# A relational graph layer's loop of 34 turns written out, with two buffers per fetched row slot and edge tables kept in DRAM

## The reference, cut to what matters

```
h = relu(layernorm(x));  x = x + sage_sum(h)       # two convolutions
h = relu(layernorm(x));  x = x + relational(h)     # the layer of this change
h = relu(layernorm(x));  x = x + attention(h)      # three attention convolutions
h = relu(layernorm(x));  x = x + sage_mean(h)      # two convolutions, batch norm

def relational(feat):              # src, dst: int (103125,), sorted by dst
    h_src = feat[src]              # etypes: 0..15; weight: (16, 64, 64)
    for r in range(16):
        msg += (h_src * (etypes == r)) @ weight[r]
    return segment_sum(msg, dst)
```

## Time and profile before

| | |
|---|---|
| median of 3 runs | 2148.41 us (2145.63 to 2152.9) |
| the profiled execution, its own time | 2156.55 us |
| its span, first to last instruction | 2154.8 us |
| PE busy | 1729.2 us (80%) |
| DVE busy | 1499.3 us (70%) |
| ACT busy | 1127.3 us (52%) |
| POOL busy | 898.3 us (42%) |
| gathers (L947), 544 for the slots | 555.8 us busy, 1022 ns each, 304.1 us idle before them |

### The profile page before, as it was taken

The page is one execution under the profiler, slowest core; times in us unless marked ns, Lnnn a source line. Parts: engine busy times, 40 slices in busy tenths (PEclk is TensorE's granted clock), DMA queues, the critical chain, the costliest instruction groups (busy, mean ns, idle before and its releaser), DMA issues. The chain is left out here.

```text
span 2154.8 us, 36900 instructions
## 1 busy us (share of the span) xinstructions
PE 1729.2 (80%) x9923; PEld 873.3 (41%) x9924; DVE 1499.3 (70%) x4058; ACT 1127.3 (52%) x2235; POOL 898.3 (42%) x828
## 2 busy tenths in 40 slices
PE   2777777883688878888887888789998998999786
PEld 0222222551344434444443444465535543544354
DVE  6999997435455666666665666478886887888854
ACT  6777776212333333333343333338885886888521
POOL 1000000005666666666666666315653654455400
PEclk9999999896799898999999899869999999999898
DMA  6000000102111111111111111220000000000000
GB/s 176 0 0 0 0 0 5 69 1 64 32 33 30 29 31 30 29 30 35 30 30 31 29 31 30 47 78 2 1 1 1 1 1 1 1 1 1 16 1 16
DMA packets 29633, 50.74 MB, mean 24 GB/s; under 512 B 12820, under 2 KB 13826, under 8 KB 29054
## 3 DMA queue, kind: packets, MB, share of 16 engines
q0 software_dynamic: 17664, 18.12, 4.9%
q1 hardware_dynamic: 11890, 31.59, 4.6%
HBM read 36.58 MB, written 7.39 MB: 20 GB/s over the span
## 5 line engine op out<-in xcount | busy, mean ns | idle before, releaser
L947 POOL DMA_INDIRECT adj<-h_table,l_idx x544 | 555.8, 1022 | 304.1 <-issue 152.4
L1138 DVE TENSOR_SCALAR adj<-adj,node_key 125x1024 f16<-125x1024 f16 x825 | 373.9, 496 | 338.5 <-PE psum L1083 153.6
L1083 PE MATMUL psum<-adj,x_sb 125*128 125x512 f16 x1650 | 446.9, 413 | 136.7 <-DVE adj L1138 122.2
L1648 POOL TENSOR_TENSOR gat_ring<-gat_ring,adj 125x750 f32<-125x750 f32 (+2 forms) x225 | 310.6, 1382 | 264.1 <-ACT gat_ring L1704 261.9
L1543 DVE SCALAR_TENSOR_TENSOR gat_ring<-x_sb,gat_node,psum 125x750 f32<-125x750 f32 (+2 forms) x375 | 317.9, 861 | 60.5 <-PE psum L1781 26.3
L1011 ACT ACTIVATE l_z<-psum 128x320 f32<-128x320 f32 x204 | 89.0, 436 | 462.3 <-remote 206.8
L1083 PEld LDWEIGHTS psum<-adj,x_sb 125*128 125x128 f16 x1650 | 162.2, 104 | 356.6 <-DVE adj L1138 165.5
L393 PE MATMUL psum<-col_hot,src_hot 128*128 128x500 bf16 x808 | 204.9, 375 | 109.8 <-DVE src_hot L322 88.7
L1778 PE MATMUL psum<-gat_ring,gat_hx 125*65 125x500 f32 (+1 forms) x500 | 242.9, 575 | 16.0 <-DVE gat_ring L1554 9.5
L319 DVE TENSOR_SCALAR col_hot<-iota_h,c_tab 128x500 bf16<-128x500 f16 x808 | 227.6, 346 | 24.7 <-PE psum L393 20.1
L1701 ACT ACTIVATE gat_ring<-gat_ring,gat_node 125x750 f32<-125x750 f32 (+2 forms) x225 | 182.2, 810 | 60.5 <-DVE gat_ring L1543 58.6
(11 more groups left out here) (260 smaller groups left out, 2298.2 us busy)
## 6 DMA issues: line engine op xcount, KB each, us to landing
adj<-h_table,l_idx POOLq DMA_INDIRECT x544
adj<-key_table SPq DMA_DIRECT2D x33, 250.0 KB
adj<-adj SPq DMA_DIRECT2D x3, 1662.5 KB
adj_saved<-adj SPq DMA_DIRECT2D x1, 3840.3 KB
adj<-adj_saved SPq DMA_DIRECT2D x5, 688.2 KB
x_sb<-in_x SPq DMA_DIRECT2D x1, 781.2 KB
x_saved<-x_sb SPq DMA_DIRECT2D x1, 781.2 KB
out<-x_sb SPq DMA_DIRECT2D x5, 156.2 KB
```

What stands on the lines that cost most here:

```text
L947: pool.indirect_dma_start(out=to[:, t, :], out_offset=None, in_=table[:, :], in_offset=bass.IndirectOffsetOnAxis(ap=index[:, t:t + 1], axi ...
L1083: last = pe.matmul(psum[:, PAIR[half] + t, :], h_parts[:, k, :], select[0:P, k % SELECTS, t * GE:(t + 1) * GE], start=(k == 0), stop=(k == ...
L1138: v.tensor_scalar(select[0:P, k % SELECTS, :], keys, node_key[:, k:k + 1], None, ALU.is_equal).then_inc(s_sel, 1)
L1648: pool.tensor_tensor(slot, slot, adj[:, k, cols(c)], ALU.mult).then_inc(s["weight_ready"], 1)
```

## The change

Every `Fori` of the relational turns becomes a Python loop, so that all 34 turns stand in the program with waits for constants. The buffer of fetched rows exists twice, for even and odd turns, with a semaphore of its own for each half and slot. The fetch for turn j therefore waits for z of turn j-2, where it waited for turn j-1, and fetch(1) has no such wait. The second half takes a tensor of its own in SBUF. To make room, d_tab and type_tab live only until the build is over: SP stores them to DRAM as the build begins, and loads them back as the relational stage begins, ahead of the keys, into the space that the one-hots use later; DVE waits for that load before it works out its table.

```diff
-        d_tab = sb("d_tab", [128, G * GT], FP32, edge_scope)[:, :]
-        type_tab = sb("type_tab", [128, G * GT], FP16, edge_scope)[:, :]
+        tab_store = nc.dram_tensor("tab_store", [128, 3 * G * GT], FP16, kind="Internal").ap()
+        tabs = sb("edge_tabs", [128, 3 * G * GT], FP16, build_scope)[:, :]
+        d_tab, type_tab = tabs[:, 0:2 * G * GT].bitcast(FP32), tabs[:, 2 * G * GT:3 * G * GT]
...
                 def _(sp):
+                    sp.dma_start(tab_store, tabs).then_inc(s_tabs, 16)
                     for loaded in (s_mats, s_mats2, s_vecs, s_x):
                         sp.wait_ge(loaded, 16)
+                    sp.wait_ge(s_tabs, 16)
...
-        got = carve(4 * GT * 2 * D).rearrange("p (g t d) -> p g t d", g=4, t=GT)
+        got_odd = sb("l1_got_odd", [128, 4, GT, 2 * D], FP16, l1_scope)[:, :, :, :]
+        got = carve(4 * GT * 2 * D).rearrange("p (g t d) -> p g t d", g=4, t=GT), got_odd
...
-        s_got = [sem(f"l1_gathered{k}", l1_scope) for k in range(4)]
+        s_got = [[sem(f"l1_gathered{half}_{k}", l1_scope) for k in range(4)] for half in range(2)]
...
+                    sp.dma_start(loaded_tabs, tab_store).then_inc(s_tabs_in, 16)
                     keys(0, 0)
                     sp.wait_ge(s_key, 16)
                     keys(1, 1)
-                    with sp.Fori(1, TURNS // 2 - 1) as q:
+                    for q in range(1, TURNS // 2 - 1):
...
                         for k in range(4):
-                            pool.wait_ge(s_z, SIX * (j - 1) + FREED[k])
+                            if not static(j, 1):
+                                pool.wait_ge(s_z, SIX * (j - 2) + FREED[k])
                             pool.sem_inc(s_tick, 1)
-                            gather(got[:, k, :, :], idx[:, half, k * GT:(k + 1) * GT], s_got[k])
+                            gather(got[half][:, k, :, :], idx[:, half, k * GT:(k + 1) * GT], s_got[half][k])
...
-                    with nc.Fori(1, TURNS // 2, engines=[ENG.Pool], head_slot={ENG.Pool: 0}) as q:
+                    for q in range(1, TURNS // 2):
                         fetch(2 * q, 0)
                         fetch(2 * q + 1, 1)
...
-                            pe.wait_ge(s_got[FETCHED[pos]], 16 * GT * (j + 1))
-                            rows = got[:, FETCHED[pos], :, :]
+                            pe.wait_ge(s_got[half][FETCHED[pos]], 8 * GT * (j + 2 - half))
+                            rows = got[half][:, FETCHED[pos], :, :]
...
-                    link(v.tensor_scalar(dw_tab, d_tab, pass_off[:, 0:1], None, ALU.subtract))
+                    dve.wait_ge(s_tabs_in, 16)
+                    link(v.tensor_scalar(dw_tab, dw_tab, pass_off[:, 0:1], None, ALU.subtract))
```

More of the change, by code:

```diff
@@ L290, in gnn @@
         square = sb("square", [128, SETS, max(ACT_TILES), 128], FP16, build_scope)
-        s_bchain, s_hot, s_sq, s_src, s_used, s_outer, s_written = (sem(n, build_scope) for n in (
-            "build_chain", "col_hots_ready", "squares_ready", "src_hots_ready", "hots_used", "outer_done", "window_written"))
+        s_tabs, s_bchain, s_hot, s_sq, s_src, s_used, s_outer, s_written = (sem(n, build_scope) for n in (
+            "edge_tabs_stored", "build_chain", "col_hots_ready", "squares_ready", "src_hots_ready", "hots_used", "outer_done", "window_written"))
         passes = nc.values_load(npass[0:1, 0:1], min_val=1, max_val=N // W + 1)
@@ L408, in gnn @@
             nc.all_engine_barrier(sems_to_clear=None)
-            for s in (s_bchain, s_hot, s_sq, s_src, s_used, s_outer, s_written):
+            for s in (s_tabs, s_bchain, s_hot, s_sq, s_src, s_used, s_outer, s_written):
                 nc.sync.sem_clear(s)
@@ L813, in gnn @@
         key_row = carve(2 * 2 * GE)
-        got = carve(4 * GT * 2 * D).rearrange("p (g t d) -> p g t d", g=4, t=GT)
+        got_odd = sb("l1_got_odd", [128, 4, GT, 2 * D], FP16, l1_scope)[:, :, :, :]
+        got = carve(4 * GT * 2 * D).rearrange("p (g t d) -> p g t d", g=4, t=GT), got_odd
         hot_space = carve(3 * GT * RW)
         hot = hot_space.bitcast(BF16).rearrange("p (s t w) -> p s t w", s=3, t=GT)
-        dw_tab = hot_space.bitcast(FP32)[:, 0:G * GT]
+        loaded_tabs = hot_space[:, 0:3 * G * GT]
+        dw_tab, type_back = loaded_tabs[:, 0:2 * G * GT].bitcast(FP32), loaded_tabs[:, 2 * G * GT:3 * G * GT]
         col_tab = carve(2 * G * GT).bitcast(FP32)
@@ L903, in gnn @@
                 "picked_T_copied", "picked_turned"))
-        s_got = [sem(f"l1_gathered{k}", l1_scope) for k in range(4)]
+        s_got = [[sem(f"l1_gathered{half}_{k}", l1_scope) for k in range(4)] for half in range(2)]
+        s_tabs_in = sem("l1_edge_tabs_in", l1_scope)
         s_first = [sem(f"l1_first_rows{k}", l1_scope) for k in range(2)]
@@ L908, in gnn @@
         x_kept = free[0:P, 0:2 * NT * D].bitcast(FP32)
-        ENG = mybir.EngineType
         LAST = TURNS - 1
@@ L963, in _ @@
                     for k in range(2):
-                        gather(got[:, k, :, :], idx[:, 0, k * GT:(k + 1) * GT], s_got[k])
+                        gather(got[0][:, k, :, :], idx[:, 0, k * GT:(k + 1) * GT], s_got[0][k])
                     pool.tensor_copy(idx_first[:, :], src_tab[:, 4 * GT:6 * GT]).then_inc(s_ix0, 1)
@@ L1035, in _ @@
                     turn(2, 0, True)
-                    with nc.Fori(1, LAST // 2 - 1, engines=[ENG.Activation], head_slot={ENG.Activation: 0}) as q:
+                    for q in range(1, LAST // 2 - 1):
                         turn(2 * q + 1, 1, True)
@@ L1044, in _, with z @@
                 def _(pe):
-                    def z(j, pos):
+                    def z(j, pos, half):
                         n = SIX * j + pos
@@ L1098, in turn @@
                         for pos, lo, hi in ((0, 0, 4), (1, 4, 8), (2, 8, 12), (3, 12, 18), (4, 18, 22), (5, 22, NT)):
-                            z(j, pos)
+                            z(j, pos, half)
                             if not static(j, LAST):
@@ L1109, in _ @@
                     turn(2, 0)
-                    with nc.Fori(1, LAST // 2, engines=[ENG.PE], head_slot={ENG.PE: 0}) as q:
+                    for q in range(1, LAST // 2):
                         turn(2 * q + 1, 1)
@@ L1198, in _ @@
                     link(v.tensor_scalar(base_row[:, :], basef_row[:, :], pass_off[0:1, 0:1], float(N), ALU.add, ALU.min))
-                    link(v.tensor_scalar(dw_tab, d_tab, pass_off[:, 0:1], None, ALU.subtract))
+                    dve.wait_ge(s_tabs_in, 16)
+                    link(v.tensor_scalar(dw_tab, dw_tab, pass_off[:, 0:1], None, ALU.subtract))
                     link(v.tensor_scalar(col_tab[:, :], dw_tab, 0.0, None, ALU.is_ge))
                     link(v.scalar_tensor_tensor(col_tab[:, :], dw_tab, float(W), col_tab[:, :], ALU.is_lt, ALU.mult))
-                    link(v.scalar_tensor_tensor(dw_tab, dw_tab, 1.0, type_tab, ALU.add, ALU.add))
+                    link(v.scalar_tensor_tensor(dw_tab, dw_tab, 1.0, type_back, ALU.add, ALU.add))
                     link(v.tensor_tensor(col_tab[:, :], col_tab[:, :], dw_tab, ALU.mult))
@@ L1208, in _ @@
                     turn(2, 0)
-                    with nc.Fori(1, LAST // 2, engines=[ENG.DVE], head_slot={ENG.DVE: 0}) as q:
+                    for q in range(1, LAST // 2):
                         turn(2 * q + 1, 1)
@@ L1224, in gnn @@
                               (nc.vector, (s_selmm, s_picked, s_pT, s_turned, s_key, s_x_back)),
-                              (nc.tensor, (*s_got, *s_first))):
+                              (nc.tensor, (*s_got[0], *s_got[1], *s_first, s_tabs_in))):
                 for done in used:
```

2 lines of the change are left out of this document (1 added, 1 removed).

## The result

The changed kernel takes 2327.43 us (median, 2319.71 to 2338.31, 4 runs) where the kernel before, beside it, takes 2149.07 (2145.63 to 2152.9, 4 runs): a ratio of 1.084, interval 1.0812 to 1.0868, 178 us slower. The forecast was 2080. The rival that holds PE's signals to the end of POOL's run had 2264 us and turns of 27 to 33 us; it was right in kind and somewhat short in size, though one of the held signals comes before the run's end. The profiled execution took 2338.31 us, with a span of 2336.5.

A forecast was written before the change was run, and what follows sets the result against it. PE was taken as closest to filling a turn, with PE and DVE waiting on late signals. -72 + 5 = -67 us from the profiled 2156.55 gave 2089.5, by the median 2081, stated as 2080; range 2017 to 2290.

The forecast's parts named there:

- What bounds the kernel now: Relational turns: PE nearest to filling a turn, idle 4.2 us per loop turn; PE and DVE wait for signals underway.
- The turn value of 23.3 us: Turns 3 to 32: each falls from 25.7 to 23.3 us, saving 72 us over 30 turns.
- The slower rival: POOL's run of 16 gathers holds PE's signals to its end: turns of 27 to 33 us, 2264 us; chance 0.43.
- Constants by themselves 0: Turns 3 to 32: constants for registers save 0 by themselves; ends nothing or 4.35 us a turn.
- The back edge 0: Relational loop: removing the loop's back edge saves 0, as no instruction packets were fetched there in 690 us.
- Two buffers: removing the waits 0: POOL's semaphore waits, 4.7 us a turn, lie off the path; removing them gives 0 directly.
- POOL's floor of 20 to 21.6 us: Relational turns: 16 gathers at 1.25 to 1.35 us each, so no turn can be shorter.
- Turn 0: +5: Turn 0: first gather run grows from 36 to 40, delaying the z signal and costing 5 us.
- The tables 0: Storing tables beside the build costs 0; loading them back, about 7 us, is hidden behind turn 0's wait: 0.
- A rule against the held signals: Skill's rule that PE and ACT never wait on anyone; by it the run of 16 could not hurt PE.

The follow-up runs named there:

- f4: Changed kernel with two POOL memsets of 128x116 after each gather, on a chip of the first kind: 2189.0 us, ratio 1.020 to the kernel before.
- j2: Changed kernel with four POOL memsets of 128x116 replacing each gather of turns 2 to 33, first kind of chip: 1958.84 us, ratio 0.912 to the kernel before.
- f1: Kernel before with all 34 turns written out, still one buffer per slot, on a chip of the first kind: 2126.29 us, ratio 0.990.
- h3: Kernel before with all turns written out, one buffer per slot, on a chip of the second kind: 2033.6 us, ratio 1.005.
- h1: Changed kernel unaltered, on a chip of the second kind: 2033.09 us, ratio 1.004 to the kernel before.
- h2: Kernel before unaltered, profiled on a chip of the second kind: 2024.48 us, beside a before of 2025.22.
- j1: Changed kernel with two POOL memsets of 128x24 after each gather, on a chip of the first kind: 2340.92 us, ratio 1.090 to the kernel before.

## Why the prediction was wrong, by its steps

**What bounds the kernel now: right.** PE and DVE wait for signals underway beside close gathers. f4 and j2 show it: with the gathers spread or gone, and all else there, no signal is late.

**The turn value of 23.3 us: the step that failed.** It was to save 72 us in turns 3 to 32; they cost 160.9 more (932.4 for 771.5). I took turns 1 and 2 of the kernel before as the nearest rows because they had constants and a run of 16. But the run of 16 that let a signal pass at 595.31 held a later one:

```profile
609.39 0.94 POOL L947 DMA_INDIRECT adj<-h_table,l_idx  x1 [0.30 <-issue]
...
604.03 0.72 PE L1062 MATMUL psum<-adj 128*128 128x320 bf16 x4
...
612.02 0.44 ACT L1011 ACTIVATE l_z<-psum 128x320 f32<-128x320 f32 x1 [2.81 <-remote]
```

The first z of turn 3, over at 604.75, was seen 7.3 us late, 1.7 us after the run. And the run was loose where it let signals pass: its first five gathers (588.36 to 594.66) started 1.58 us apart in the mean, with one of 2.28, where those of turn 12 after, up to 916.60, were 1.31 apart. So these turns were held too, only less, and were no measure of a regular run of close gathers. In the changed kernel POOL's start is tied to ACT's indices, and these to a z signal that the run itself held: turn for turn the run starts behind the same signal, lies over positions 5, 0, 1 and 2, and delays those of 1 to 3; the first 5 us of it let signals pass (position 0, 0.3 us). The regular row, the loop's own run of 8 with 6.5 us late, was the better guide to a regular pattern.

**The slower rival: its mechanism shown, its size near.** It put a hold of 12 us in a turn of 29.4. The hold at position 2 is 11.9 us, to 2.1 us after the run; with 3.7 at position 1, which ends within the run, and 1.4 at position 3 the turn is 31.1. That the hold was 12 is luck in part: it was the middle of a wide range (8.4 to 17.4).

**Constants by themselves 0: small miss.** They save 21 us on this kind of chip (f1), within the ends given, and cost 8 on the other (h3).

**The back edge 0: not separated.** It went with the constants in f1 and h3. More code was fetched, 72 and 55 packets against 46 and 33 in f1 too, which was the faster all the same. So the Trainium skill's advice to unroll fully (Runtime: NRT & Kernel Launch, Instruction fetch mechanics) is neither borne out nor refuted as to fetches; 8 us more on chips of the second kind speak against it.

**Two buffers: removing the waits 0, right.** h1 and h3 differ by 0.5 us, where no signal is held. POOL's floor of 20 to 21.6 us is right too: 21.7 in h2.

**Turn 0: +5 was too small.** The first run was to be 40 gathers and was 56 (8, two short casts, 48), because the indices for turn 2 came before the run ended and fetch(2) joined it. Turns 0 to 2 cost 30.6 + 57.1 + 30.2 = 117.9 us against 89.5, 28 more.

**The tables 0: right.** PE's first z came at 513.7 us for 514.5.

**A rule against the held signals.** The Trainium skill, SBUF — State Buffer, Who interferes with whom, has PE and ACT wait on nobody. On chips of the second kind the traces agree: in h1 ACT follows the z matmuls by 0.03 us beside unbroken gathers. On those of the first it does not, by 11.9 us, though what is held is a signal and not an access: PE itself goes on to its next matmuls meanwhile.

**The change in signs.** +161 in turns 3 to 32, +28 in turns 0 to 2, -8 in the rest: 181, against 181.7 between the two spans.

Open: the exact spacing at which the hold begins, what in the chip holds the signals, and why some chips do not show it. Nor does any run tell whether the recording of signals for the profile has a part in it: every execution on record has a recorded span and clock, and none is known to have run unrecorded. A version that spaces gathers about 1.45 us apart and pauses nowhere else was not run on a chip of the first kind. Of the whole kernels run, f1 is the fastest there, at 0.990; on the second kind none beats the kernel before.

## What to carry to other kernels

A wait that is off the critical path can still be the pause that lets other engines' signals through: before buffers are doubled to remove it, ask what unbroken run of DMA issues takes its place, and read the delay between an operation's end and its waiter's start inside such a run. A regular pattern of the loop is to be extrapolated from the loop's own rows, not from a few turns before it, and rows that seem free are to be read to the end of the run. And a gain or loss that rests on late signals is to be measured on several chips; here one program stood at 1.084, 1.004 and 1.002 of the same kernel.

## What the runs showed of the hardware

Chips differ by 6% on the same program: the kernel before took 2146.88 and 2146.68 us on two and 2023.3, 2025.22 and 2024.64 on three others. The difference lies where the gathers are: turns 3 to 32 take 771.5 us before and 651.5 in h2, turns 0 to 2 take 89.5 and 75.9, together 134 us, for spans that differ by 132. The gathers are issued alike (1.25 us apart at the closest on both kinds), and the data move alike: a gather's last packet is through 1.17 us (median) after the gather's end in the changed kernel of the result and 1.19 in h1. From 905 to 936 us the gathers' queue in the changed kernel, first on the chip of the result:

```profile
q0 software_dynamic: 512, 0.53, 10.1%
```

then in h1:

```profile
q0 software_dynamic: 736, 0.76, 15.6%
```

That is 32 packets a gather in both (16 and 23 gathers), and 31 us x 16 x 10.1% / 512 = 98 ns a packet on the one against 105 on the other. But the page of h1 tells how long a gather took to land (2.6 us), and that of the result does not. After:

```profile
adj<-h_table,l_idx POOLq DMA_INDIRECT x272
```

h1:

```profile
adj<-h_table,l_idx POOLq DMA_INDIRECT x272, 2.6
```

The trace of the result kept 2017 of the 8832 landing records (16 a gather, 552 gathers), that of the kernel before 3204 and that of h1 all 8832. A missing record is not a late signal: f4 kept 6086, and nothing was late in its turns. So the page says nothing of when the landing signals came on the first kind.

The data are on time, and PE's signals are not. It is not signals in general either. In the result's trace, 64 of the 191 records of s_z and 226 of the 660 of s_selmm during the gathers came over 0.5 us behind the matmul that raised them, and none of ACT's (404 kept of 584) or of DVE's (956 of 1185), which all stand 0.01 us behind their instruction. Of POOL's own memsets in j1, 10 of 220 kept records came over 0.5 us behind. That late signals queue behind those of closely spaced gathers would fit PE and POOL, but not ACT and DVE as far as their records are kept; the cause stays open.
